# A two-layer graph network on one core: narrow and wide products of the sums in turn, gathers released by the sums

## What is computed

```python
h = x projected to 64 scalars and 32 vectors per node      # per node
w = silu(edge_scalars @ W_fc1) @ W_fc2                     # per edge, 192 or 224 numbers
g = h[edge_src]                                            # gather, one row per edge
mid_s = concat(w0 * gs * e_s, w3 * sum_c(gv * e_v))        # 64 + 32
mid_v = concat(w1 * gs * e_v, w2 * gv * e_s)               # (64 + 32) x 3 components
# layer 1 also: w5 * cross(gv, e_v), another 32 x 3
agg = segment_sum(concat(mid_s, mid_v), edge_dst)          # 6250 rows
x = layernorm(x + self_part(x) + project(agg))             # layer 1 with silu and sigmoid gates
```

## Time and profile before

| | us |
|---|---|
| median of 3 runs | 4455.87 (4447.93 to 4457.54) |
| the profiled execution | 4453.04 |
| its span, first to last instruction | 4451.0 |

### The profile page before, as it was taken

How to read it: one execution, slowest core, us unless ns; L and a number is a source line. 1 busy time by engine, 2 the same in 40 slices (tenths; PEclk the granted TensorE clock), 3 DMA queues, 4 the chain that set the end, 5 groups by cost and what they waited for, 6 DMA issues and landing times. The chain is left out here.

```text
span 4451.0 us, 166762 instructions
## 1 busy us (share of the span) xinstructions
PE 4044.4 (91%) x58000; PEld 3053.2 (69%) x58001; DVE 2847.8 (64%) x7746; ACT 2961.5 (67%) x12216; POOL 3054.0 (69%) x3215
## 2 busy tenths in 40 slices
PE   7888888888888888888979999999999999999987
PEld 4677777777777777776756766666666666666666
DVE  4544444444444444444667888888888888888878
ACT  1566666666666666665337877777777777777753
POOL 2577777777777777776017777777777777777751
PEclk9999999999999999999889999999999999999995
DMA  4222222222222222223334444444444444444433
GB/s 107 71 72 73 72 72 72 72 73 73 72 73 73 72 72 72 72 73 68 104 98 129 121 120 120 122 121 120 121 121 121 121 121 121 122 121 121 121 100 94
DMA packets 356348, 430.11 MB, mean 97 GB/s; under 512 B 203298, under 2 KB 248648, under 8 KB 356112
## 3 DMA queue, kind: packets, MB, share of 16 engines
q0 software_dynamic: 156288, 329.79, 27.4%
q1 hardware_dynamic: 199618, 98.11, 8.2%
q10 hardware_dynamic: 400, 1.68, 0.1%
HBM read 405.56 MB, written 23.74 MB: 96 GB/s over the span
## 5 line engine op out<-in xcount | busy, mean ns | idle before, releaser
L415 POOL DMA_INDIRECT e_rows<-scratch_table,e_index x3136 | 2967.3, 946 | 1010.5 <-issue 926.2
L438 ACT ACTIVATE e_match<-e_match,e_attr 128x40 f32<-128x40 f32 x10976 | 2480.9, 315 | 176.3 <-DMA e_attr<-in_edge_attr 172.1
L470 PEld LDWEIGHTS e_sum<-e_match,e_msg 128*64 128x64 f32 (+1 forms) x50176 | 1714.0, 125 | 698.3 <-DVE e_msg L629 244.3
L470 PE MATMUL e_sum<-e_match,e_msg 128*64 128x40 f32 (+2 forms) x50176 | 1846.2, 223 | 247.5 <-DVE e_msg L626 194.6
L461 PE MATMUL e_w<-k_fc,e_hidden 100*128 100x192 f32 (+1 forms) x4704 | 1275.2, 407 | 0.0
L618 DVE TENSOR_TENSOR e_msg<-e_w,e_rows 128x512 f32<-128x512 f32 x784 | 537.8, 686 | 1008.1 <-DMA e_rows<-scratch_table,e_index 980.0
L461 PEld LDWEIGHTS e_w<-k_fc,e_hidden 100*128 100x128 f32 (+1 forms) x4704 | 833.0, 190 | 385.3 <-issue 364.8
L431 ACT ACTIVATE e_hidden<-e_h 100x512 f32<-100x512 f32 (+1 forms) x784 | 384.4, 490 | 925.9 <-PE e_h L450 921.2
L450 PE MATMUL e_h<-e_inputs,k_fc 128*100 128x512 f32 (+1 forms) x1568 | 708.6, 534 | 57.9 <-DMA e_inputs<-in_inputs 27.0
L608 DVE TENSOR_TENSOR e_misc<-e_misc,e_rows 128x384 f32<-128x384 f32 x392 | 221.8, 566 | 354.2 <-DMA e_rows<-scratch_table,e_index 354.1
L624 DVE TENSOR_TENSOR e_msg<-e_w,e_rows 128x384 f32<-128x384 f32 x784 | 428.1, 546 | 0.0
(11 more groups left out here) (122 smaller groups left out, 1454.0 us busy)
## 6 DMA issues: line engine op xcount, KB each, us to landing
e_rows<-scratch_table,e_index POOLq DMA_INDIRECT x3136
e_inputs<-in_inputs SPq DMA_DIRECT2D x196, 256.0 KB
e_attr<-in_edge_attr SPq DMA_DIRECT2D x392, 24.0 KB, 1.7
e_inputs<-in_inputs SPq DMA_DIRECT2D x196, 40.0 KB
e_index<-in_src SPq DMA_DIRECT2D x392, 4.0 KB
scratch_self<-m_h SPq DMA_DIRECT2D x10, 480.0 KB, 4.5
f_self<-scratch_self POOLq DMA_DIRECT2D x10, 480.0 KB, 5.0
m_xrow<-in_x POOLq DMA_DIRECT2D x10, 400.0 KB, 5.0
```

Source lines behind the costliest of these rows:

```text
L415: pool.indirect_dma_start(out=rows[j][:, t, :], out_offset=None, in_=table_dram, in_offset=bass.IndirectOffsetOnAxis(ap=index[q][:, c:c + ...
L438: last = nc.scalar.activation(match[j][:, t, c, :], match[j][:, t, 4, :], ACT.Copy, scale=attr[q][:, e0 + t, e:e + 1])
L470: return nc.tensor.matmul(out[rows, c0:c0 + n, :], m[:, t, f:f + rows.stop - rows.start], m5[:, t, which:which + n, :], start=(first and t ...
```

## The change

The file is rewritten in most places. What bears on the time:

- **The sums.** `window_sums` becomes `tile_sums`, which issues all products of one tile before the next tile's. The messages are laid out so that all four chunks of the window are used, and every product is 32 wide, except that the first two scalar blocks are joined to one product of 64 (array columns 0 to 63): one with three matches, one with one. Layer 0 has 8 products per tile, layer 1 has 14.
- **The gathers** wait for `sum_done` of the group four before instead of `msg_done`, index buffers are four instead of two, and the loop covers eight groups.
- **Layer 1's weights.** Four products with 64 rows and 256 columns (upper and lower half of the rows) in place of two with 128 rows and 480; the cross product comes from two more products of the gathered rows, and the sums put it together (a column block with the opposite sign).
- **Nodes' own part.** In 50 of the 98 bodies, TensorE adds two products (`base`) behind the sums of one group and VectorE adds them to a tensor `nodes` kept in SBUF (`node_terms`); SyncE loads the rows for it and in layer 1 stores `self1`.
- **Setup.** All node loads up front, five PSUM buffers, half tiles paired so that every product has 128 rows, no float copy of the destinations; `dst_rel` stays in SBUF, the table of windows is made on 98 partitions.
- **Node stages.** TensorE reads the sums directly, without the copy; fewer and fuller weight matrices; statistics interleaved over several tiles; GpSimd clears the sums tile by tile; the last normalization runs on ScalarE in batches with the stores behind it.

The core of the diff:

```diff
-                for t in range(TPG):
-                    product(t, slice(0, 64), 0, 64, 0, n=3, first=True, end=(L == 0))
-                    product(t, slice(64, 128), 2, 0, 3, first=True)
-                    product(t, slice(64, 128), 0, 128, 3)
-                    if L == 1:
-                        product(t, slice(0, 64), 3, 320, 4, end=True)
-                        product(t, slice(64, 128), 3, 384, 4)
-                for t in range(TPG):
-                    product(t, slice(64, 96), 1, 192, 3, end=True)
-                    for c in range(3):
-                        last = product(t, slice(96, 128), 1, 224 + V * c, c, end=(c == 2))
+            def tile_sums(out, m, m5, opens, closes):
+                def product(g, c0, f, which, n=1, first=False, end=False, cols=32):
+                    return nc.tensor.matmul(out[32 * g:32 * g + cols, c0:c0 + n, :], m[:, f:f + cols],
+                                            m5[:, which:which + n, :], start=first and opens, stop=end and closes)
+                product(0, 0, 64, 0, n=3, first=True, cols=S)
+                product(2, 0, 128, 3, first=True)
+                product(3, 3, 224, 0, first=True)
+                if L == 0:
+                    product(2, 1, 160, 3)
+                    product(3, 3, 256, 1)
+                    product(0, 3, 0, 3, end=True, cols=S)
+                    product(2, 2, 192, 3, end=True)
+                    return product(3, 3, 288, 2, end=True)
+                product(2, 1, 160, 3)
+                product(3, 0, 352, 2)
+                product(0, 3, 0, 3, end=True, cols=S)
+                product(2, 2, 320, 1)
+                product(3, 0, 480, 1)
+                product(2, 2, 448, 0)
+                product(3, 1, 384, 0)
+                product(2, 3, 256, 1)
+                product(3, 1, 416, 2)
+                product(2, 3, 288, 2, end=True)
+                return product(3, 2, 192, 3, end=True)
```

```diff
                 for u in range(TPG // layer.tiles_per_product):
-                    c0, n = u * layer.tiles_per_product * WPITCH, w[f"fc2_{L}"].shape[1]
-                    last = nc.tensor.matmul(ps_w[j % 2][:, c0:c0 + n], hidden[j % 2][:, u * P:(u + 1) * P], w[f"fc2_{L}"][:, :],
-                                            start=True, stop=True)
+                    for h in range(layer.tiles_per_product):
+                        c0, k = (u + 2 * h) * WPITCH, fc2.shape[0] // layer.tiles_per_product
+                        last = nc.tensor.matmul(ps_w[j % 2][:, c0:c0 + n], hidden[j % 2][k * h:k * h + k, u * P:(u + 1) * P],
+                                                fc2[k * h:k * h + k, :], start=True, stop=True)
...
+                for t in range(TPG):
+                    last = tile_sums(ps_sum[j % 2], msg[j % 2][:, t, :], match[j][:, t, :, :], t == 0, t == TPG - 1)
+                if with_base:
+                    last = base(i)
+                last.then_inc(sum_done, 1)
...
-                pool.wait_ge(msg_done[j], count)
+                    pool.wait_ge(sum_done, summed[GPB * parity + j])
...
+                summed = [2 * GPB * pair + (o - GPB + 1) for o in range(2 * GPB)]
```

## The result

| | us | against the kernel before |
|---|---|---|
| before, on the same chip | 4456.70 (4447.93 to 4457.57) | 1 |
| after, median of 4 runs | 5524.70 (5523.79 to 5525.83) | 1.2402 [1.2381, 1.2423] |
| forecast | 5565 (4200 to 5950) | |

The kernel after is slower by 24%, 40 us under the forecast. The first view is again the table of windows by stage: us, then busy time (count) of PE, PEld, DVE, ACT and POOL, the granted clock, DMA share and GB/s. The stretches are setup, the gathers of layer 0, the sums behind them, the nodes of layer 0, the gathers of layer 1, the sums behind them, and the tail.

What follows compares the result with a forecast made beforehand. Issue of gathers bound the edge stages at 5.00 us a group; shape changes would make TensorE the bound at 6.53 and 6.73 us. 4453 + 628 + 701 - 218 = 5564, forecast 5565 us, range 4200 to 5950.

Steps and rivals of the forecast that it cites:

- The price of a change: Sums on TensorE: each change of array-piece shape drains it for 0.13 us, 16 per group where there were 2.
- The blocks of a tile of layer 0: Layer 0 sums: runs of same-width products in a tile, 0.33, 0.27, 0.25 and 0.20 us, together 1.05 us.
- The rest of a group: TensorE's hidden product and edge weights: 2.33 us in layer 0, 1.65 in layer 1 instead of 2.24 (up to 2.45).
- the fourth rival: Layer 1's edge weights: row halves do not overlap, +310 us, 5880 us; its chance is included in the main mechanism's 0.76.
- The edge stages: Gather stages of both layers: TensorE becomes the bound, 2600 and 2676 us with their ends, +628 and +701.
- Outside the edge stages: Setup -73 us, node stage of layer 0 -95, tail -50: together -218 us.
- The sum: Whole kernel: 4453 + 628 + 701 - 218 = 5564, forecast as 5565 us.
- Signs named ahead: Profile after: GpSimd waits for sums, 6.5 to 6.7 us per four gathers; load-free slices between products; edge stages about 2600 us.
- A: Layer sums: a tile's 64-wide product of 120 columns, put at 0.33 us with its shape change.
- Z: Layer sums: a tile's 64-wide product of 40 columns, put at 0.25 us with its shape change.
- the third rival: TensorE's granted clock falls in the edge stages, adding some 20%: 6500 us; chance 0.03.
- The rival of free changes: Sums: shape changes cost nothing where pieces do not overlap, gathers stay the bound, only -218 us remains: 4235 us; chance 0.18.

Runs made afterwards that it cites:

- The four kernels above: Kernel after (16 changes of shape per group, 5525 us) and its same products reordered to 2, 4 and 8: 4185, 4312 and 4684 us.
- the all-32 kernel: Kernel after with its two 64-wide products per tile split into two of 32 each: 4150.19 us, 0.9326 of before; 0.86 on another chip.
- 8 changes: Kernel after with each tile's wide products issued together, then its narrow ones: 4683.69 us, 1.0527 of before; 0.9551 on another chip.

## Why the prediction was right, point by point

**The price of a change.** Forecast 0.13 us, taken from two fixed parts of phases; measured 0.12 to 0.134. The blocks of a tile of layer 0 were put at 0.33, 0.27, 0.25 and 0.20 us and measure 0.35, 0.27, 0.24 and 0.19. The sums of a group: 4.20 and 5.08 forecast, 4.20 and 5.06 measured. The Trainium skill, "TensorEngine Tiling (Array Packing)", section Tiling Modes, Key Properties, says that changing the mode, and not only the tile, drains TensorE; here it holds for pieces of two widths in different columns, at 0.13 us.

**The rest of a group.** 2.33 forecast and 2.34 measured in layer 0; 1.65 and 1.69 in layer 1. That the row halves run side by side was a guess from the column groups, with 2.45 us as its other end; it was right. In layer 1 the eight passes of a group's weights take the second window here, behind the hidden product in the first:

```profile
3829.40:3830.00 0.60, 0.60 (x6) 1.00 0.03 8
3830.00:3831.09 1.09, 1.09 (x9) 1.00 0.02 1
```

The eight take 1.09 us; one after the other they would take 8 x 0.214 = 1.7. So the fourth rival falls.

**The edge stages.** Forecast 2600 and 2676 us with their ends, measured 2581.8 + 18.5 = 2600 and 2695.5 + 21.0 = 2717. Layer 0's groups with the nodes' own part are 0.65 us longer (7.19 against 6.54 at the median), where 0.6 was forecast. Layer 1 has 41 us more than forecast. In its second half, where no group carries a node part, TensorE still stops once per turn of the loop before the hidden product. Its waits in that half (waited for, us in total, times, longest):

```profile
PE e_h L587 <- issue: 18.1, 47, 0.5
PE e_h L587 <- DMA e_inputs<-in_inputs: 5.3, 1, 5.3
```

That is 18 us for the turns and 5 for one late transfer; another late transfer in the first half is 8 us, and a period of 6.76 in place of 6.73 gives 392 x 0.03 = 12. Together they are 43 us. The first loop has no such stops; why, I do not know.

**Outside the edge stages**, the term that was mis-sized. Forecast -218, made of -73, -95 and -50. Measured -86 (51.8 us to the first gather), -143 (85.9 us from the last sum to layer 1's first gather) and -70 (68.4 us of tail): -298 with the fractions. The direction was right in all three. Between the layers the price of a pass was taken as 0.16 us and the two ends as 23 us. The 14 passes a tile are there, 700 in all, but in the middle of the stage TensorE is busy without a pause, with 451 passes in flight in 50 us, 0.111 us each:

```profile
2660.00:2710.00 50.00, 50.00 (x451) 50.00 (x451) 33.69 (x146) 26.71 (x70) 17.33 (x33) 1.00 0.37 121
```

That makes 78 of the 85.9 us. In the kernel before a pass of this stage took 0.21 us (175 us for 820). Three things differ: its passes had up to 320 columns, now at most 128; they had 96, 64 and 128 rows in turn, now 128 throughout; and the granted clock was 0.87, now 0.98. How much each gives no run separates. The tail was put at 1.5 us a tile by VectorE's steps; VectorE is busy 53.7 us for the 50 tiles, about 1.1 us each. In setup the forecast took 0.9 us a tile from a pass of the tail at a clock of 0.58, although setup itself has 1.00 in the earlier trace rows.

**The sum.** 2600.3 + 2716.5 + 51.8 + 85.9 + 68.4 = 5522.9, the span. The errors are nothing in layer 0, +41 us in layer 1 and -80 outside, together -40. That the whole misses by so little is in part luck: an overrun and a larger saving cancel by half.

**A slip that did no harm.** The prediction let the gathers hide the changes up to (5.00 - 3.45) / 16 = 0.10 us each. That takes the sums as if wide and narrow products still ran side by side between changes. By its own blocks layer 1 has 5.08 - 16 x 0.13 = 3.0 us of sums without any change, and 5.00 - 3.0 - 1.65 leaves 0.35 us, 0.02 us a change. The four kernels above bear that out (5.06 - 16 x 0.13 = 3.0). So at 0.09 us a change the time would by the same terms have been near 5000 us already, and 0.10 us is no border between faster and slower.

**Signs named ahead.** GpSimd idle before gathers by the sums, in groups of four, each 6.54 and 6.76 us: seen. Holes of the weight loads between A, the narrow products and Z: seen. The granted clock of the edge stages stayed at 1.00 and 0.99, so the third rival falls as well. The three times outside, 65, 133 and 88 us, were said to hold in either case and did not: they are 51.8, 85.9 and 68.4.

**The rival of free changes**, at 4235 us, fell by its mechanism, but its other half was real: with no change to pay the kernel takes 4150 us, faster than before by 6.7%.

## What to carry to other kernels

Read the order of array shapes as a cost of its own: each step between products of different width costs TensorE 0.13 us here, so eight products in alternating widths cost more than ten of one width. Joining two 32-wide products into one of 64 saved no time at all (sorted by width the kernel takes 4185 us, with 32-wide products alone 4150); where widths must differ, issue all of one width and then all of the other, over as many tiles as the PSUM order allows. And a stage that is bound by something else hides such a cost completely up to its slack (here 5.00 - 2.33 - 1.38 = 1.3 us a group), and not at all beyond it: work out the slack first, then count the changes.

## What the runs showed of the hardware

- A change of the width of the array piece costs 0.12 to 0.134 us also where the two pieces share no column, in both layers and in two layouts of the products.
- Products of one width in four column groups run side by side: 80 passes in 1.38 us, 17 ns each. Row halves of 64 rows do so too: eight passes of 256 columns in 1.09 us, where one after the other they would take about 1.7.
- On two other chips TensorE stops inside long runs of small matmuls (2445 times in the all-32 kernel, 0.73 us from start to start at the median), the granted clock is lower (0.84 for 0.985), and the kernel before takes 7530 us in place of 4450. The ranking of variants is not the same there: 8 changes are slower than before in the one place (1.053) and faster in the other (0.955).
